# First layer of a two-layer kernel: where the target product lives, and in which order PE serves a step

## The reference, cut to what matters

```python
# B=4 sequences of 512 tokens, H=16 heads of HD=64, chunks of K=64 tokens
def step(carry, inp):
    W, bb = carry
    xq_c, xk_c, xv_c = inp
    lr = sigmoid(einsum('bhkc,hcd->bhkd', xk_c, theta) + tb)
    eta = token_eta * (lr / HD)
    Z1 = xk_c @ W + bb                         # "state product", keys
    x_hat = (Z1 - Z1.mean(-1)) / sqrt(Z1.var(-1) + EPS)
    grad_output = g * x_hat + be - (xv_c - xk_c)
    gxh = grad_output * g
    grad_x = (HD * gxh - gxh.sum(-1) - x_hat * (gxh * x_hat).sum(-1)) / (HD * std)
    Wn = W - einsum('bhkc,bhkd->bhcd', eta * xk_c, grad_x)   # "gradient product" dW
    bn = bb - (eta * grad_x).sum(-2)                         # "bias product"
    Zq = xq_c @ Wn + bn                        # "state product", queries
    out = xq_c + g * normalised(Zq) + be
    return (Wn, bn), out
# then out @ wo; the router of the next part takes the best 32 tokens of each
# of 16 experts and sequence: logits = x @ Wg, top-k over tokens, softmax
```

## Time and profile before

| | us |
|---|---|
| median of 3 runs (946.74 to 947.41) | 946.85 |
| the profiled execution, its own time | 945.96 |
| its span, first to last instruction | 944.2 |
| the first layer's loop, z(0) to the last att product | 34.6 to 317.2 |
| PE busy over the span | 888.2 (94%) |
| DVE busy over the span | 770.7 (82%) |
| ACT, POOL busy over the span | 554.7, 635.6 |

### The profile page before, as it was taken

How to read it: one execution, slowest core, us unless ns; L and a number is a source line. 1 busy time by engine, 2 the same in 40 slices (tenths; PEclk the granted TensorE clock), 3 DMA queues, 4 the chain that set the end, 5 groups by cost and what they waited for, 6 DMA issues and landing times.

```text
span 944.2 us, 19724 instructions
## 1 busy us (share of the span) xinstructions
PE 888.2 (94%) x7768; PEld 612.3 (65%) x7768; DVE 770.7 (82%) x1180; ACT 554.7 (59%) x833; POOL 635.6 (67%) x579
## 2 busy tenths in 40 slices
PE   2898999999998899999999999999999999999997
PEld 2666787877776688655665666666665665665564
DVE  7779898899886637788888888888888888879876
ACT  4554566666664363665766655756656666666662
POOL 4567788888884050956955966955966965866872
PEclk9598999999999899899999999999999999999999
DMA  8100000000000500110210220110120110120110
GB/s 220 42 2 2 2 2 3 2 2 3 2 2 2 154 26 23 57 57 10 66 49 25 71 75 8 60 57 24 65 77 10 57 64 20 61 77 20 45 51 24
DMA packets 24964, 38.27 MB, mean 41 GB/s; under 512 B 9316, under 2 KB 15480, under 8 KB 22824
## 3 DMA queue, kind: packets, MB, share of 16 engines
q1 hardware_dynamic: 23240, 34.74, 12.1%
q10 hardware_dynamic: 1632, 2.27, 0.8%
HBM read 28.29 MB, written 1.43 MB: 31 GB/s over the span
## 4 chain that ended last, share of the span: by engine, by line
PE 60%; DVE 22%; issue 11%; POOL 3%; ACT 3%; DMA 1%; SPq 0%; POOLq 0%; DVEq 0%
PE bank L1162 12%; PE bank L1164 10%; PE bank L1163 10%; DVE hdh L957 6%; PE bank L1319 3%; PE bank L1435 3%; PE quad L1467 3%; PE quad L1211 3%; DVE add L966 3%; DVE mx L950 2%; PE quad L1202 2%; PE quad L1370 2%; PE bank L1276 2%; PE bank L1486 1%; PE quad L1291 1%
## 5 line engine op out<-in xcount | busy, mean ns | idle before, releaser
L950 DVE TENSOR_REDUCE mx<-quad 128x4 f32<-128x2048 f32 x64 | 146.3, 2286 | 38.5 <-PE quad L1467 38.4
L1130 POOL CAST hdh<-xn 128x512 fp32r<-128x512 f32 x96 | 65.7, 684 | 155.3 <-ACT xn L627 155.3
L644 ACT ACTIVATE ex<-quad 128x2048 f32<-128x2048 f32 x64 | 120.6, 1884 | 58.8 <-PE quad L1477 58.8
L1132 POOL TENSOR_TENSOR hdl<-hd,hdh 128x512 fp32r<-128x512 f32 x96 | 129.6, 1350 | 7.7
L1132 POOL TENSOR_TENSOR hdl<-xn,hdh 128x512 fp32r<-128x512 f32 x96 | 128.8, 1342 | 7.7
L1162 PE MATMUL bank<-hdh,W2h 128*128 128x512 f32 x256 | 113.5, 443 | 5.7 <-DVE hdl L960 4.7
L627 ACT ACTIVATE xn<-bank,b1c 128x512 f32<-128x512 f32 x128 | 87.8, 686 | 28.5 <-POOL hdl L1132 19.7
L627 ACT ACTIVATE hd<-bank,b1c 128x512 f32<-128x512 f32 x112 | 76.9, 687 | 43.8 <-PE bank L1164 26.9
L1163 PE MATMUL bank<-hdh,W2l 128*128 128x512 f32 x256 | 101.1, 395 | 0.0
L1164 PE MATMUL bank<-hdl,W2h 128*128 128x512 f32 x256 | 101.0, 395 | 0.0
L1162 PE MATMUL bank<-cH,W1h 128*128 128x512 f32 x192 | 80.9, 422 | 0.7 <-DVE cL L977 0.7
(11 more groups left out here) (303 smaller groups left out, 2188.7 us busy)
## 6 DMA issues: line engine op xcount, KB each, us to landing
cwB<-gate_rows SPq DMA_DIRECT2D x16, 1024.0 KB, 4.6
kx<-kqh SPq DMA_DIRECT2D x32, 64.0 KB, 2.1
qx<-kqh SPq DMA_DIRECT2D x32, 64.0 KB, 2.1
W1r<-in_L_ffn_W SPq DMA_DIRECT2D x1, 1024.0 KB, 10.7
kx<-kql SPq DMA_DIRECT2D x16, 64.0 KB, 2.1
qx<-kql SPq DMA_DIRECT2D x16, 64.0 KB, 2.1
rec<-rec_rows SPq DMA_DIRECT2D x32, 32.0 KB, 2.1
out<-fin SPq DMA_DIRECT2D x4, 256.0 KB, 2.3
```

The lines of the kernel that those rows point to most:

```text
L644: act.activation(ex[:, t % 2, :, :], quad[:, :, :], ACT.Exp, scale=float(AD) ** -0.5).then_inc(ROUND["exps_ready"], 1)
L950: dve.tensor_reduce(mx[:, t, :, 0], quad[:, :, :], AX_X, ALU.max, negate=True).then_inc(ROUND["score_max"], 1)
L1130: pool.tensor_copy(hdh[:, m % RING, :], tile(n)).then_inc(ROUND["pool_split"], 1)
L1132: pool.tensor_tensor(hdl[:, m % RING, :], tile(n), hdh[:, m % RING, :], ALU.subtract).then_inc(ROUND["pool_split"], 1)
```

## The change

The target product no longer goes to first_bank and is no longer copied by ACT. It is written in two halves of 256 columns into columns 256 to 511 of quad banks 0 and 1, beside the gradient product, and DVE's gradient reads it there. Each half is four matmuls of 256 columns (before, four of 512 in all). Because both products share banks, target(s) waits for update(s-3) and gradient(s-1), and gradient(s) waits for dW(s-2).

PE's order in a step becomes: XK_, bias_rows, state_q, state, queries, target, dW(s-2), in odd steps bias, att, keys, turn. In step 0: bias_rows, state, XK_.

Ahead of the loop: the transposes of wq and the router's logits move from step 1 to before the bias and the rates (the rates go to second_bank); the router's Wg is loaded ahead of W1 in SP's queue and padded by POOL before it splits wk; POOL no longer waits for the centred weights; POOL splits wq in step 0 between scaled(0) and gx_xhat(0); DVE splits wu before the rates and makes the target's row (gbr) last. In the loop: the top-32 search starts in step 0 and is spread over steps 0 to 6, the exponential is in step 1, the output weights in step 3, wo is scaled by ACT in steps 4 and 5 (8 activations), the ranks are turned in step 7, the b3 copies move from step 6 to step 8.

```diff
-        dwb = quad[:, 0:2, :]
+        dwb = quad[:, 0:2, 0:256]
+        U = quad[:, 0:2, 256:512]
@@ sync
+            sp.dma_start(wg0[:, :], A["L0_ffn_Wg"]).then_inc(w0_loaded, 16)     # after wk, ahead of W1
@@ scalar
             keys(0, 1, first_bank)
             keys(1, 2, second_bank)
+            act.wait_ge(wq_turned, 1)
+            for n in range(2):
+                act.activation(wqT[:, 4 * n:4 * n + 4, :], bank[n][:, :]..., ACT.Copy).then_inc(wq_turned_taken, 1)
+            act.wait_ge(wu_ready, 2)
+            act.activation(wuh[:, :], wu[:, :], ACT.Copy, scale=1.0 / HD).then_inc(wu_high, 1)
             act.wait_ge(bias_placed, 1)
             act.activation(Bhl[:, :], db_[:, :], ACT.Copy).then_inc(bias_first_high, 1)
...
-            def take_u(s):
-                if s in LIVE:
-                    act.wait_ge(CHUNK["u_ready"], s + 1)
-                    act.activation(U[:, s % 4, :], first_bank[:, :], ACT.Copy).then_inc(CHUNK["u_taken"], 1)
...
-                take_xk(s), take_turned(s - 2), squares(s), squares_q(s), take_u(s)
+                if s == 0:
+                    squares(0), take_xk(0)
+                else:
+                    take_xk(s), take_turned(s - 2), squares(s), squares_q(s)
                 if s % 2:
                     bias_high((s - 3) // 2)
                 deviation(s)
...
+                if s in (4, 5):
+                    act.wait_ge(wo_loaded, 16 * 5)
+                    for a in range(4 * (s - 4), 4 * (s - 3)):
+                        last = act.activation(wog[:, a, :], wo[:, a, :], ACT.Copy, scale=gam[:, a:a + 1])
+                    last.then_inc(wog_ready, 1)
@@ vector
                     dve.wait_ge(CHUNK["scaled_ready"], s + 1)
-                    dve.wait_ge(CHUNK["u_taken"], s + 1)
-                    dve.tensor_tensor(gx[:, u, :], t1[:, u, :], U[:, u, :], ALU.add).then_inc(CHUNK["gx_ready"], 1)
+                    dve.wait_ge(CHUNK["u_ready"], s + 1)
+                    if s >= 2:
+                        dve.wait_ge(CHUNK["dw_ready"], s - 1)
+                    dve.tensor_tensor(halves(gx[:, u, :]), halves(t1[:, u, :]), U, ALU.add).then_inc(CHUNK["gx_ready"], 1)
...
+                if s != 2:
+                    centre(s - 1)
+                sum_squares(s), sum_squares_q(s)
+                if s == 1:
+                    without_eight(0)
+                rdev(s), xhat(s)
                 if s == 0:
-                    rates_scaled()
+                    rates_scaled(), router_logits()
+                elif s == 1:
+                    best_eight(1)
+                elif s == 2:
+                    best_eight(3)
+                elif s == 3:
+                    without_eight(3)
+                elif s == 4:
+                    chosen()
+                elif s == 5:
+                    ranks_in_order()
+                elif s == 6:
+                    ranks_of_chosen()
                 rdev_q(s)
                 if s % 2:
                     bias_low((s - 3) // 2)
                 normed(s), rate_of(s - 1), gradient(s), update(s - 2), sum_gx(s)
+                if s == 0:
+                    best_eight(0)
+                elif s == 1:
+                    without_eight(1)
...
+                elif s == 6:
+                    router_weights()
+                sum_gx_xhat(s)
                 if s == 1:
+                    centre(1), best_eight(2), without_eight(2)
@@ gpsimd
-                scaled(s), gx_xhat(s), rated(s - 1), part(s), less(s)
-                if s == 2:
-                    pool.wait_ge(wo_loaded, 16 * 5)
-                    pool.tensor_tensor(wog[:, :, :], wo[:, :, :], ..., ALU.mult).then_inc(wog_ready, 1)
+                scaled(s)
+                if s == 0:
+                    pool.wait_ge(wq_high, 1)
+                    pool.tensor_tensor(wql[:, :], wq[:, :], wqh[:, :], ALU.subtract).then_inc(wq_low, 1)
+                gx_xhat(s), rated(s - 1), part(s), less(s)
@@ tensor
-                    pe.wait_ge(CHUNK["keys_taken"], (1, 3)[s] if s < 2 else keys_through(s - 1))
+                    if s > 2:
+                        pe.wait_ge(CHUNK["state_updated"], s - 2)
                     if s:
-                        pe.wait_ge(CHUNK["u_taken"], s)
-                    pe.matmul(first_bank[:, :], ones[:, :], gbr[:, ws], start=True, ...)
-                    mm3(first_bank[:, :], two(xth, i, g), two(xtl, i, g), wuh[:, ws], wul[:, ws], start=False)...
+                        pe.wait_ge(CHUNK["gx_ready"], s)
+                    for k in range(2):
+                        wc = slice(hf * 512 + 256 * k, hf * 512 + 256 * k + 256)
+                        pe.matmul(U[:, k, :], ones[:, :], gbr[:, wc], start=True, stop=False, ...)
+                        last = mm3(U[:, k, :], two(xth, i, g), two(xtl, i, g), wuh[:, wc], wul[:, wc], start=False)
+                    last.then_inc(CHUNK["u_ready"], 1)
...
             for s in range(4 * NC + 6):
-                XK_(s), bias_rows(s), state_q(s), state(s), target(s)
-                if s % 2:
-                    bias((s - 3) // 2)
-                if s == 6:
+                if s:
+                    XK_(s), bias_rows(s), state_q(s), state(s)
+                else:
+                    bias_rows(0), state(0), XK_(0)
+                if s == RANKS:
...
-                queries(s), att(s - 2), keys(s), dW(s - 2)
+                queries(s), target(s), dW(s - 2)
+                if s % 2:
+                    bias((s - 3) // 2)
+                att(s - 2), keys(s)
                 turn(s - 1)
```

More of the change, by code:

```diff
@@ new lines, in router_logits, with best_eight @@
+            def router_logits():
+                dve.wait_ge(choice_logits, 1)
+                dve.wait_ge(moe_loaded, 16 * N_M)
+                dve.tensor_scalar(lgt[:, :], misc[0:BE, :], bg0[:, :], None, ALU.add).then_inc(choice_step, 1)
+                dve.wait_ge(choice_step, 1)
+            def best_eight(k):
+                link(dve.max(m8[:, k, :], lgt[:, :] if k == 0 else wrk[:, :]))
+                if k == 0:
+                    dve.tensor_scalar(es[:, 0:1], m8[:, 0, 0:1], -1.0, None, ALU.mult).then_inc(choice_step, 1)
@@ new lines, in without_eight, with chosen, ranks_in_order, ranks_of_chosen @@
+            def without_eight(k):
+                link(dve.match_replace(wrk[:, :], m8[:, k, :], lgt[:, :] if k == 0 else wrk[:, :], -3.0e38))
+            def chosen():
+                dve.wait_ge(choice_exp, 1)
+                link(dve.tensor_tensor(wrk[:, :], lgt[:, :], wrk[:, :], ALU.not_equal))
+            def ranks_in_order():
+                link(dve.tensor_tensor_scan(lgt[:, :], wones[:, :], wrk[:, :], 0.0, ALU.mult, ALU.add))
+            def ranks_of_chosen():
+                dve.tensor_tensor(rkp[:, 0, :], lgt[:, :], wrk[:, :], ALU.mult).then_inc(ranks_ready, 1)
@@ L1051, in _ @@
             pool.tensor_tensor(th[:, :], th[:, :], wk[:, :], ALU.mult).then_inc(theta_scaled, 1)
+            pool.wait_ge(w0_loaded, 48)
+            pool.wait_ge(wg_ready, 1)
+            for b in range(B):
+                last = pool.tensor_copy(wgP[:, b, b * E0:(b + 1) * E0], wg0[:, :])
+            last.then_inc(wg_ready, 1)
             pool.wait_ge(wk_high, 1)
@@ L1178, in _ @@
             features(second_bank, 1, 0, wkh, wkl).then_inc(CHUNK["keys_ready"], 1)
+            pe.wait_ge(xn_turned_taken, B)
+            pe.wait_ge(wq_loaded, 16)
+            for a in range(NP):
+                last = pe.transpose(bank[a // 4][:, a % 4 * P:(a % 4 + 1) * P], wq[:, a * P:(a + 1) * P], ident)
+            last.then_inc(wq_turned, 1)
+            pe.wait_ge(wg_ready, 2)
+            for b in range(B):
+                last = pe.matmul(misc[0:BE, :], wgP[:, b, :], xnT[:, b * S:(b + 1) * S], start=(b == 0), stop=(b == B - 1), skip_group_check=True)
+            last.then_inc(choice_logits, 1)
             pe.wait_ge(bias_ready, 1)
@@ L1184, in _ @@
                 for b in range(B):
-                    last = pe.matmul(misc[b % 2 * 64:b % 2 * 64 + 64, (i * 2 + b // 2) * H:(i * 2 + b // 2 + 1) * H],
+                    last = pe.matmul(second_bank[b % 2 * 64:b % 2 * 64 + 64, (i * 2 + b // 2) * H:(i * 2 + b // 2 + 1) * H],
                                      xnT[:, b * S + i * K:b * S + (i + 1) * K], Th[:, :], start=True, stop=True, skip_group_check=True)
@@ L1284, in dW @@
                         pe.wait_ge(CHUNK["state_updated"], s)
-                    else:
-                        pe.wait_ge(wq_turned_taken, 2)
                     for a in range(4):
@@ L1341, in _ @@
                     features(second_bank, 3, 0, wkh, wkl).then_inc(CHUNK["keys_ready"], 1)
-                    pe.wait_ge(wq_loaded, 16)
-                    for a in range(NP):
-                        last = pe.transpose(bank[a // 4][:, a % 4 * P:(a % 4 + 1) * P], wq[:, a * P:(a + 1) * P], ident)
-                    last.then_inc(wq_turned, 1)
-                    pe.wait_ge(wg_ready, 2)
-                    pe.wait_ge(rates_biased, 1)
```

(5 more changed lines are left out.)

104 lines of the change are left out of this document (35 added, 69 removed).

## The result

The changed kernel took 959.77 us (954.87 to 961.61, 4 runs) against 947.13 us (946.74 to 947.61, 4 runs) of the kernel before: ratio 1.0123, 95% interval 1.0093 to 1.0152. It is slower, as forecast, but by 12.6 us instead of 6, and outside the range (947.5 to 957.5). The profiled execution took 960.33 us, its span is 958.5 (944.2 before). Of the four executions one took 954.87, at a mean granted clock of 0.974; the others lie between 0.968 and 0.970.

What follows compares the result with a forecast made beforehand. PE was taken to bound the loop's middle, with a second path through bias_high and normed ending equally late; something else bounds the start. 7.0 + 2.0 - 4.4 + 1.5 = +6.1 on 945.96 gives 952.1 profiled, median 953.0 us, range 947.5 to 957.5.

Steps and rivals of the forecast that it cites:

- Direction and mechanism: Steady loop: bias product 1.2 us later delays deviation, normed and bias_rows in steps with s % 4 of 3; kernel slower.
- +7.0: Steady loop, step 11 to step 31: 1.4 us lost per four-step cycle, five times, from late bias product and keys.
- Faster: Rival: in steps with s % 4 of 3 the bias product's delay does not reach bias_rows; about 944 us, chance 0.13.
- Target in two halves, and from PSUM: Steady loop: halves cost 0 to +0.1 us a step; gradient reading PSUM costs 0, against the skill's 62 cycles.
- The clock: Loop: each cycle's new 1.2 us stall may halve PE's clock, one drop in five or six: +1.5 us (0 to 7.5).
- Clock in every cycle: Rival: each new stall in the loop drops the clock, +7.5 us instead of +1.5, 959 us; chance 0.08.
- The end of the loop: Steps 31 to 33: later bias products and dW(30) waiting for rated ahead of att, +2.0 us (0.9 to 3.0).
- The start: Steps before z(11): work moved to where PE waits brings z(11) 4.4 us earlier (2.5 to 7), the least certain term.

Runs made afterwards that it cites:

- e7: Changed kernel with PE's order in a step as before the change (target, bias product, queries, att, keys, dW): 944.96 us, ratio 0.9986.
- e4: Kernel before, target in its own bank and copied by ACT, with dW ahead of att and the bias product behind dW: 963.62 us, ratio 1.0177.
- e5: Changed kernel in its own order, useless matmuls filling PE's stalls in steps 12, 16, 20, 24 and 28: 952.22 us, ratio 1.0066.
- e1: Changed kernel with ACT calling deviation ahead of bias_high in odd steps: 952.20 us, ratio 1.0063.
- e11: Changed kernel with PE's order as before the change from step 32 on (bias product, queries, att, dW): 958.00 us, ratio 1.0092.
- e8: Changed kernel: bias product behind target, keys (and their copy) first, deviation ahead of bias_high, ranks turned in step 10, att ahead of dW from step 32: 947.63 us.
- e9: Changed kernel with PE's order chosen step by step, ranks turned in step 8, ACT's deviation ahead of bias_high: 943.45 us, ratio 0.9972.
- e12: Steps 0 to 7 as in e9, PE's order as before the change from step 8, ranks turned in step 8, deviation ahead of bias_high: 943.12 us.
- e10: e7 with the ranks turned in step 8 instead of 7 and ACT's deviation ahead of bias_high: 943.66 us, ratio 0.9970.
- e2: Kernel before with ACT calling deviation ahead of bias_high in odd steps: 942.77 us, ratio 0.9958.
- e3: Changed kernel with PE's order in odd steps target, bias product, queries, dW: 950.86 us, ratio 1.0046.

## Why the prediction was wrong

*Direction and mechanism: right.* The bias product moved behind queries and dW, and each step of the chain came where the text put it: 2.34 for 2.3, 3.44 for 3.4, normed's end 6.50 for 6.6, idle PE 1.25 for 1.2, cycle 32.01 for 32.0. e7 shows this order as the cause (with the old one the changed kernel takes 944.96), e4 that it needs no move of the target. Where PE stood idle differs: 0.56 ahead of bias_rows, and 0.69 ahead of XK_, for ACT's copy of the keys, which stands behind bias_high and deviation_q in ACT's queue and was late with them. From z(11) to z(31) waits cost 7.2 us (e5's 159.96 less 152.75) against +7.0. One detail failed: the path to normed went through ACT's deviation_q as well as deviation, as e1 showed; the rival "Faster" would therefore not have come out at 944 even with deviation free (e1: 952.20).

*Target in two halves, and from PSUM: right.* gradient took 685 ns (23 of them), xhat with its one PSUM operand 692 ns beside it:

```profile
L779 DVE TENSOR_TENSOR arena<-quad,sm 128x512 f32<-128x512 f32 x23 | 15.9, 692 | 0.8
L795 DVE TENSOR_TENSOR arena<-arena,quad 128x512 f32<-128x512 f32 x23 | 15.8, 685 | 0.1
```

The rule of the Trainium skill ("VectorE: DVE Perf Modes", the TRN2 errata) that was weighed there, 62 cycles more for a PSUM source, does not show; the measurement decides.

*The clock: the step that failed.* "One drop in five or six such stalls: +1.5" measured 6.0 in the loop. Two rows of the kernel before, one with a drop and one without, were read as one drop in five or six stalls, with nothing behind that number; they bore one in two at best. It was four in five in the profiled execution, and eleven in fifteen with e4 and e11, whose stalls are the same. The rival "Clock in every cycle", 959, was nearly what happened, and I gave it 0.08. That the drops need PE's idle time, and don't come from the order or the other engines alone, e5 shows. The range took that case in by its chance only, and ended at 957.5.

*The end of the loop: under-sized.* +2.0 (0.9 to 3.0) measured +5.2. e11 gives 3.3 of it to the order from step 32 on. In the changed kernel dW(30) ahead of att waits 0.75 for rated, and turn, right behind att, waits twice for ACT's copy of it (0.55 at 307.64 and at 314.83), which dW covers in e11:

```profile
301.83 1.13 PE L1338 MATMUL quad<-arena 64*64 64x64 f32 x32 [0.75 <-POOL arena L1136]
314.83 0.63 PE L1355 MATMUL bank<-cst,arena 128*128 128x128 f32 x4 [0.55 <-ACT attnT L531]
```

And PE runs 13.6 us at half clock behind z(31), against 10.2 in e11 and 6.8 before. The text counted 0.5 for the first wait, and neither the waits of turn nor the clock. Of the other 1.9, 0.7 lie in step 31, where bias_rows comes 6.70 after z(31) instead of 6.01 (the text had 0.85); the rest was not taken apart, but e11's 3.4 us more at half clock than before lie in it.

*The start: right within its bounds, in part by luck.* -3.5 for -4.4, but out of terms that missed both ways. Step 0's squares came 0.2 earlier, not 2; gradient(2) started at 55.91 (55.65 before), not at 54.4; gradient(6) at 89.68, not at 88.0; z(7) came at 92.99, not at 90, about when DVE was through with the ranks, so that step 7 gave back less than the 2.5 that were counted. With the ranks turned in step 7 z(11) lay near 126 in every order. In e8, e9 and e12, which turn them later and hold other edits too, it lay at 122.3 to 123.4, in e10 at 126.09, with the half-clock stretch of step 3 in it.

Together the misses are 0.9 + 0.2 + 4.5 + 3.2 - 0.5 behind the loop = 8.3, which takes 952.1 to 960.4; the profiled execution took 960.33.

*Not settled.* Why the stall of step 19, and in e4 those of steps 15 and 27, equal in their waits, were spared, and why equal waits in step 3 brought a drop in e10 and none in e7; where e2 gains; and what each part of the new start is worth, since no run took it apart.

## What to carry to other kernels

When an order is changed to cover one wait, follow every engine's queue behind each moved instruction: here a product moved back by 1.2 us held two paths of ACT, and the keys that covered a copy were missed as soon as they stood elsewhere. A stall of about 1 us in a PE-bound loop can cost more than twice itself through the clock, so a repeated one is priced with a drop in most cases (eleven of fifteen here) unless rows say otherwise, and the range is left wide enough for all of them; useless matmuls in the gap are a cheap test, and a way out. Changes between small and full tiles are counted too, at some 0.1 us each here.

## What was not expected of the hardware

- Two waits of 0.69 and 0.56 us in one step were followed by 3.4 us at 1.2 GHz in eleven cases of fifteen (4 of 5 after, 3 of 5 in e4, 4 of 5 in e11), at 1.5 us each; waits of 0.50 and 0.40 (e1) and below (e3, e7, e9) in none of the five cycles of the profiled executions.
- The same waits in the same step of two nearly equal programs, 1.16 and 0.53 us in e7, 1.15 and 0.51 in e10, went with full clock in one and with 6.8 us at half clock in the other.
- The executions of one program fell in two groups some 8 us apart, with mean clocks of 0.978 to 0.980 and of 0.969 to 0.971 (e11).
- PE is busy 30.38 us in a cycle of e7 and 30.83 in one of e9 with the same matmuls in another order.
